# An attention stage on one core: a new order inside each step, value projections in the output bank, and the weighing of values split by query blocks

## The reference, cut to what matters

```python
x = x + 0.5 * ffn(layernorm(x), router_w, gate_w, up_w, down_w)     # 8 experts, top 2
x = x + attn(layernorm(x), W_qkv, W_out)
x = x + 0.5 * ffn(layernorm(x), router_w, gate_w, up_w, down_w)

def attn(x, W_qkv, W_out):                  # x: 8 sequences of 512 tokens, width 128, fp32
    q, k, v = split(x @ W_qkv)              # 16 heads of 64
    q, k = rotary(q), rotary(k)
    s = where(lower_triangle, q @ k.T / 8, -1e9)
    return concat_heads(softmax(s) @ v) @ W_out
```

## Time and profile before

| | |
|---|---|
| time, median of 3 runs | 1277.3 us (1276.87 to 1278.48) |
| profiled execution, first to last instruction | 1277.2 us |
| PE busy | 1203.9 us, 94% |
| DVE busy | 903.4 us, 71% |
| POOL busy | 814.4 us, 64% |
| ACT busy | 795.7 us, 62% |
| first and last matmul of `scores` start (line 2003) | 270.3 us, 1012.7 us |

### The profile page before, as it was taken

The page is one execution under the profiler, slowest core; times in us unless marked ns, Lnnn a source line. Parts: engine busy times, 40 slices in busy tenths (PEclk is TensorE's granted clock), DMA queues, the critical chain, the costliest instruction groups (busy, mean ns, idle before and its releaser), DMA issues. The chain is left out here.

```text
span 1277.2 us, 26829 instructions
## 1 busy us (share of the span) xinstructions
PE 1203.9 (94%) x8070; PEld 891.3 (70%) x8070; DVE 903.4 (71%) x1995; ACT 795.7 (62%) x2264; POOL 814.4 (64%) x888
## 2 busy tenths in 40 slices
PE   7799999979999999999999999999999879999992
PEld 6588888856666666666666666666666568888882
DVE  6775344358888888888788987798998767533543
ACT  4665665646667666767676677766656656555552
POOL 4233356158778788788777776677666536766662
PEclk8899999979999999999999999999999969999996
DMA  9034122122222221222222222212212051114223
GB/s 325 26 96 156 53 57 70 40 66 54 61 46 47 59 59 41 52 59 52 47 52 53 58 54 54 67 34 51 51 36 49 17 180 41 49 48 114 61 63 109
DMA packets 87753, 86.44 MB, mean 68 GB/s; under 512 B 11249, under 2 KB 78705, under 8 KB 87233
## 3 DMA queue, kind: packets, MB, share of 16 engines
q1 hardware_dynamic: 76640, 65.50, 19.9%
q0 software_dynamic: 8864, 18.17, 5.3%
q10 hardware_dynamic: 2112, 1.05, 0.3%
HBM read 33.43 MB, written 17.69 MB: 40 GB/s over the span
## 5 line engine op out<-in xcount | busy, mean ns | idle before, releaser
L1915 POOL TENSOR_SCALAR at_prob<-at_prob,at_rec 128x128 f32<-128x128 f32 (+3 forms) x256 | 312.0, 1223 | 167.6 <-DVE at_rec L2117 165.7
L2297 ACT ACTIVATE at_prob<-at_s,at_nb 128x128 f32<-128x128 f32 (+3 forms) x512 | 264.7, 535 | 16.5 <-DVE at_nb L2109 12.9
L2308 ACT ACTIVATE at_probT<-at_pt 128x128 f32<-128x128 f32 (+3 forms) x256 | 105.2, 437 | 227.5 <-PE at_pt L2022 227.5
L790 POOL DMA_INDIRECT f_xb<-xn_dram,f_source x142 | 141.2, 994 | 161.8 <-PE f_b L1285 101.6
L2109 DVE TENSOR_REDUCE at_nb<-at_s 128x2 f32<-128x256 f32 (+3 forms) x256 | 203.3, 815 | 10.6 <-PE at_s L2008 10.6
L1447 DVE TENSOR_TENSOR f_hid<-f_b,f_silu 128x512 f32<-128x512 f32 x142 | 98.5, 693 | 136.5 <-PE f_b L1298 100.0
L2103 DVE TENSOR_TENSOR at_turned<-at_pj,rope 128x1024 f32<-128x1024 f32 x122 | 148.7, 1219 | 56.5 <-PE at_pj L1969 52.8
L2022 PE MATMUL at_pt<-ident,at_prob 128*128 128x128 f32 x1280 | 183.6, 276 | 4.1 <-DVE wts L381 1.0
L2003 PE MATMUL at_s<-at_KT,at_QT 64*128 64x128 f32 (+3 forms) x1024 | 176.0, 462 | 4.0 <-DMA at_KT<-at_probT 2.8
L1909 POOL TENSOR_TENSOR at_R<-at_turned 128x512 f32<-128x512 f32 x126 | 157.4, 1269 | 24.0 <-DVE at_turned L2103 24.0
L2034 PE MATMUL at_o<-at_probT,at_V 128*64 128x512 f32 (+3 forms) x1024 | 152.0, 437 | 10.9 <-ACT at_probT L2315 3.3
(11 more groups left out here) (326 smaller groups left out, 2224.4 us busy)
## 6 DMA issues: line engine op xcount, KB each, us to landing
at_QT<-at_R SPq DMA_DIRECT2D x128, 128.0 KB, 2.4
at_KT<-at_R SPq DMA_DIRECT2D x124, 128.0 KB, 2.4
ys_dram<-y SPq DMA_DIRECT2D x71, 64.0 KB, 1.8
f_down<-down_t SPq DMA_DIRECT2D x2, 2048.0 KB, 9.2
xn_dram<-f_xn SPq DMA_DIRECT2D x12, 256.0 KB, 6.8
f_xb<-xn_dram,f_source POOLq DMA_INDIRECT x142, 2.6
X<-x SPq DMA_DIRECT2D x4, 512.0 KB, 6.1
gate<-gate_t SPq DMA_DIRECT2D x8, 256.0 KB, 5.1
```

Of the source, the lines that this page charges most:

```text
L790: pool.indirect_dma_start(out=xb[j % AHEAD][:, :], out_offset=None, in_=xn_dram, in_offset=bass.IndirectOffsetOnAxis(ap=routing.source[:, ...
L1915: pool.tensor_scalar(w, w, rec[:, q, 1:2], None, ALU.mult).then_inc(probB_ready, 1)
L2297: act.activation(prob[q][:, h, :], s_bank[q % 2][:, h, 0:n], ACT.Exp, bias=nb[:, q, h:h + 1], scale=1.0, accum_out=sums[:, q, h:h + 1]).th ...
L2308: act.activation(probT[0][:, 0:q + 1, q * P:(q + 1) * P], pt_bank[0][:, at:at + (q + 1) * P].rearrange("p (b r) -> p b r", r=P), ACT.Copy) ...
```

## The change

On PE, the quarter of `values` moves behind the third transposed block and goes to `o_bank` instead of `pj`; it waits for the output of the step before to be copied out of that bank, and `weigh` waits for its copy. The second half of `project` moves from the end of a step to the next step, behind the first transposed blocks. The second scores move in front of `out_project`, and the turns of the input behind both. `weigh` is then the last thing in a step, directly in front of the next scores, and it runs in two parts: query blocks 0 to 2, when those are copied, and then block 3. On DVE the first two maxima stand together at the start, inverting is split from scaling (`invert`) and goes ahead of the copies, the second `rotate` follows the first two copies, the statistics and the first two scalings come before `maximum(i, 2)`, and `residual` comes between `maximum(i, 2)` and `maximum(i, 3)`. On ACT the exponentials of blocks 0 and 1 follow each other, and that of block 2 comes before the copies of block 3. POOL's and SP's lists are as they were.

```diff
@@ -1970,12 +1970,13 @@
 
                 def values(w, t):
                     b, half = w // 2, w % 2
-                    if w == 0 and t % 2:
-                        wait(pe, v_ready, t - 1)
-                        bank = o_bank[:, :]
-                    else:
+                    if w == 0 and t % 2 == 0:
                         projection_bank(v_ready, 4 * w + t + 1)
                         bank = pj[:, :]
+                    else:
+                        wait(pe, v_ready, 4 * w + t - 1)
+                        wait(pe, ot_ready, 4 * (w - 1) + t)
+                        bank = o_bank[:, :]
                     rows = slice(t * P, (t + 1) * P)
                     cols = slice(2048 + half * 512, 2048 + (half + 1) * 512)
                     hi, lo = XT[b % 2][:, 0, rows], XT[b % 2][:, 1, rows]
@@ -2027,13 +2028,22 @@
                     j = i % 8 % 4
                     pe.wait_ge(v_ready, 4 * (i // 4) + 4)
                     wait(pe, ot_ready, i)
+
+                    def heads(b, first, last, start, stop):
+                        for h in range(2):
+                            one = pe.matmul(o_bank[64 * h:64 * h + 64, first:last],
+                                            V[(i // 4) % 2][:, b, 128 * j + 64 * h:128 * j + 64 * h + 64],
+                                            probT[h][:, b, first:last], start=start, stop=stop)
+                        return one
+
+                    pe.wait_ge(ptA_ready, 4 * i + 3)
+                    pe.wait_ge(ptB_ready, 4 * i + 3)
+                    for b in range(3):
+                        heads(b, b * P, 3 * P, b == 0, False)
                     pe.wait_ge(ptA_ready, 4 * i + 4)
                     pe.wait_ge(ptB_ready, 4 * i + 4)
                     for b in range(4):
-                        for h in range(2):
-                            one = pe.matmul(o_bank[64 * h:64 * h + 64, b * P:SEQ],
-                                            V[(i // 4) % 2][:, b, 128 * j + 64 * h:128 * j + 64 * h + 64],
-                                            probT[h][:, b, b * P:SEQ], start=(b == 0), stop=(b == 3))
+                        one = heads(b, 3 * P, SEQ, False, b == 3)
                     one.then_inc(pv_psum, 1)
 
                 for n in range(EARLY):
@@ -2044,6 +2054,7 @@
                         values(0, 2 * n - 1)
                 for i in range(STEPS + 2):
                     this, last = i < STEPS, 0 < i <= STEPS
+                    valued = i > 0 and values_of(i)[0] < HALVES
                     if this:
                         scores(i, 0)
 
@@ -2057,8 +2068,8 @@
                         routing.count_tokens(pe, 0, pt_bank[0][:, 3 * P:4 * P], pt_bank[1][:, 3 * P:4 * P])
                     if last:
                         turn_probs(i - 1, (0, 1))
-                    if i > 0 and values_of(i)[0] < HALVES:
-                        values(*values_of(i))
+                    if 0 < i and i - 1 + EARLY < ROTATIONS:
+                        project(i - 1 + EARLY, 1)
                     if i in LEAD_JUDGED:
                         pe.wait_ge(lead.logits_ready, LEAD_JUDGED[i] + 1)
                     if i == LEAD_COUNTED:
@@ -2066,17 +2077,23 @@
                         pe.wait_ge(routing.gap_ready, 1)
                     if last:
                         turn_probs(i - 1, (2,))
+                    if valued:
+                        values(*values_of(i))
+                    if this:
+                        scores(i, 2)
+                    if i >= 2:
+                        out_project(i - 2)
+                    if valued:
+
+                        last_value = 4 * values_of(i)[0] + values_of(i)[1] + 1
                     if i in TURN:
-
+                        pe.wait_ge(v_ready, last_value)
                         pe.wait_ge(ot_ready, i - 1)
                         prep.turn(pe, TURN[i], o_bank)
                     if i in LEAD_TURNED:
+                        pe.wait_ge(v_ready, last_value)
                         pe.wait_ge(ot_ready, i - 1)
                         lead.turn(pe, LEAD_TURNED[i], prep.xn, o_bank)
-                    if i >= 2:
-                        out_project(i - 2)
-                    if this:
-                        scores(i, 2)
                     if last:
                         turn_probs(i - 1, (3,))
                     if i + EARLY < ROTATIONS:
@@ -2085,10 +2102,10 @@
                         pe.wait_ge(prep.lo_ready, TURN[i])
                     if i in LEAD_TURNED:
                         pe.wait_ge(lead.xts_ready, LEAD_TURNED[i] + 1)
+                    if valued:
+                        pe.wait_ge(v_ready, last_value)
                     if last:
                         weigh(i - 1)
-                    if i + EARLY < ROTATIONS:
-                        project(i + EARLY, 1)
 
             @block.vector
             def _(dve):
@@ -2109,12 +2126,15 @@
                     dve.tensor_reduce(nb[:, q, :], s_bank[q % 2][:, :, 0:(q + 1) * P], axis=AX, op=ALU.max,
                                       negate=True).then_inc(nb_ready, 1)
 
+                def invert(i, q):
+                    Q = 4 * i + q
+                    dve.wait_ge(exp_ready, 2 * Q + 2)
+
+                    wait(dve, probB_ready, Q - 3)
+                    dve.reciprocal(rec[:, q, :], sums[:, q, :]).then_inc(rec_ready, 1)
+
                 def normalise_a(i, q):
                     Q = 4 * i + q
-                    dve.wait_ge(exp_ready, 2 * Q + 2)
-
-                    wait(dve, probB_ready, Q - 3)
-                    dve.reciprocal(rec[:, q, :], sums[:, q, :]).then_inc(rec_ready, 1)
                     dve.wait_ge(rec_ready, Q + 1)
                     w = prob[q][:, 0, :]
                     dve.tensor_scalar(w, w, rec[:, q, 0:1], None, ALU.mult).then_inc(probA_ready, 1)
@@ -2239,37 +2259,40 @@
                     rotate(n, 1)
                 for i in range(STEPS + 2):
                     this, last = i < STEPS, 0 < i <= STEPS
-                    if 0 < i and i - 1 + EARLY < ROTATIONS:
-                        rotate(i - 1 + EARLY, 1)
                     if this:
                         maximum(i, 0)
+                        maximum(i, 1)
                     if last:
-                        normalise_a(i - 1, 3)
-                    if last:
+                        invert(i - 1, 3)
                         copy_b(i - 1, 0)
                         copy_b(i - 1, 1)
                     if i == LEAD_COUNTED:
                         lead_counted(i)
-                    if this:
-                        maximum(i, 1)
+                    if 0 < i and i - 1 + EARLY < ROTATIONS:
+                        rotate(i - 1 + EARLY, 1)
                     if last:
+                        normalise_a(i - 1, 3)
                         copy_b(i - 1, 2)
                     lead_first(i)
+                    if this:
+                        invert(i, 0)
+                        normalise_a(i, 0)
+                        invert(i, 1)
+                        normalise_a(i, 1)
+                    if i in MEASURE:
+                        prep.moments(dve, MEASURE[i])
+                    if this:
+                        maximum(i, 2)
                     if i >= 2:
                         residual(i - 2)
-                    if i in MEASURE:
-                        prep.moments(dve, MEASURE[i])
+                    if this:
+                        maximum(i, 3)
                     if i in TURN:
                         prep.trailing(dve, TURN[i], o_bank)
-                    if this:
-                        normalise_a(i, 0)
-                        normalise_a(i, 1)
-                        maximum(i, 2)
-                    if this:
-                        maximum(i, 3)
                     if i + EARLY < ROTATIONS:
                         rotate(i + EARLY, 0)
                     if this:
+                        invert(i, 2)
                         normalise_a(i, 2)
                     if i < 4:
                         shares(i)
@@ -2283,7 +2306,7 @@
                     if w >= 2 and t == 0:
 
                         act.wait_ge(pv_psum, 4 * (w - 1))
-                    bank = o_bank if w == 0 and t % 2 else pj
+                    bank = pj if w == 0 and t % 2 == 0 else o_bank
                     act.activation(V[w % 2][:, t, :], bank[:, :], ACT.Copy).then_inc(v_ready, 1)
 
                 def exponent(i, q):
@@ -2335,20 +2358,21 @@
                         lead.judged(act, LEAD_JUDGED[i], pt_bank[0][:, 3 * P:4 * P])
                     if this:
                         exponent(i, 0)
+                        exponent(i, 1)
+                    if last:
+                        copy_a(i - 1, 2)
                     if i > 0 and values_of(i)[0] < HALVES:
                         values(*values_of(i))
                     if this:
-                        exponent(i, 1)
+                        exponent(i, 2)
                     if i in TURN:
```

(6 more changed lines are left out.)

## The result

The changed kernel takes 1294.3 us, the median of four runs (1290.8 to 1295.5), against 1277.1 for the kernel before: a ratio of 1.013, 95% interval 1.0115 to 1.0145. It is slower by 17 us; the forecast was 1298. The profiled execution is the shortest of the four, 1290.8 us, with a span of 1289.0.

The account below looks back on a forecast made before the run. PE was taken to set the pace, with DVE only 2.2 us a step to spare. Some 60 steps x 0.13 = 7.8, with 5.6 + 5 + 2.7, made 21 us: 1277.2 + 21 = 1298 us, range 1260 to 1322.

Parts of the forecast that it names:

- The chain: Ordinary attention step from first scores: DVE's held scalings delay `maximum(i, 2)`, `residual` and `project`; 11.71 us, 0.13 more than before.
- The new wait: PE, ready at 7.6 to 8.1 us of the step, waits for `residual`; `project`'s first half starts at 8.49.
- the lower bound: POOL's additions cannot start before the second `rotate` ends: 4.03 to 6.52 us of the step, which then takes 11.53.
- The extras: Moved extra work, seven steps of each kind: `MEASURE` 5.6 us, `TURN` 5, `LEAD_MEASURED` 2.7; routing work counted as no difference.
- The split: PE's `weigh` in two parts: worth 0.76 us a step in the new order, its six added pairs taken at 0.02.
- (a): Rival: DVE's first scaling cannot slip between POOL's two additions; 42 us slower, 1319 us; chance 0.22.
- the seam: Point between POOL's two additions, at 5.46 us of the step, where DVE's scaling of block 0 runs, ending at 5.55.
- (b): Rival: DVE's scalings are not held; step 11.19 us, 1265 us, chance 0.20; full form about 1243 us, chance 0.04.
- (c): Rival: no difference; POOL's additions at their lower bound and half of the extras, +3 us, 1280 us; chance 0.08.
- (d): Rival: POOL's scaling also holds DVE's second scaling; 12.5 us a step, about 1340 us; chance 0.03.
- the prediction's reason against it: In the kernel before, DVE's scaling at 614.49 runs its 0.35 us unhurt inside POOL's scaling from 614.27.

## Why the prediction was right

**The chain.** Predicted and measured times in the ordinary step, t = 0 at the first scores: second `rotate` 2.76, 2.71; additions 4.21 to 6.70, 4.01 to 6.67; scaling of block 0 from 4.97 to 5.55, 4.89 to 5.53; scaling of block 1 until 6.86, 6.82; `maximum(i, 2)` 6.78, 6.74; `residual` done 8.34, 8.29; `project` 8.49, 8.34; `weigh` 9.39, 9.23; next scores 11.71, 11.55. The new wait, its place and both of its causes are as forecast. That `residual`, by way of the held scalings, sets the step is shown by the version that moves them and nothing else.

**What was mis-sized in it.** The restart of `project` behind `residual` took 0.05 us, not the 0.15 that I had from a wait of PE for ACT. With small errors ahead of it (0.05 by the end of `residual`) this makes 0.16 a step, some 9 us over the stage. Two errors inside cancelled: POOL's scaling of block 3 took 1.56 and not 1.85, so the additions began at the lower bound; but the pair took 2.66 and not 2.49, since DVE's scaling of block 3 was under way when it began.

**The extras.** From the starts of the scores in both traces, step by step: the seven `MEASURE` steps are longer by 5.6 us together (predicted 5.6), the seven `TURN` steps by 5.7 (5), the seven `LEAD_MEASURED` steps by 2.7 (2.7). Seventeen other steps from 36 on, mostly with routing work, add 4.4, where I had counted nothing; 21 ordinary ones give back 0.5, the first two 2.6, and the last two add 0.4. The sum is 15.7 to 15.8. How the 17 us between the medians divide beyond that is not shown by two traces that are 11.8 apart. The `TURN` steps are longer for the reason forecast: `weigh` waits for the subtraction and starts at 10.22 of the step (predicted 10.33).

```profile
605.97 0.48 PE L1967 MATMUL at_pj<-at_XT,w_hi 128*128 128x512 f32 x1
...
607.79 2.39 PE L2034 MATMUL at_o<-at_probT,at_V 128*64 128x384 f32 x28 [0.87 <-DVE even_XT L1754]
```

So the three kinds of extras were sized rightly, 14.0 against 13.3 us, and with the routing steps they are the whole loss. That the total of 1298 came out within 4 us is partly luck: the ordinary step, forecast 0.13 longer than before, is 0.03 shorter, which makes the forecast 9 us too high, and the routing steps that it left out make it 4 too low.

**The split.** Predicted at 0.76 us a step in the new order, measured 0.83; its six added pairs at 0.02, measured 0.02.

**The rivals.** (a), the seam lost, did not happen, and the kernel with one addition shows that the seam matters: it costs 13 us to take it away. It is less than the 21 that (a) gave, because the single addition ends at 6.53 of the step, where (a) went by a pair that ends at 6.70; the second scaling is free in both. (b), scalings that are not held, did not happen; its step of 11.19 us is what the version with moved scalings reaches, 11.14. (c) was nearest for the ordinary step: the additions began at 4.01 where it had 4.03, and the step took 11.55 where it had 11.53; it missed by counting half of the extras.

(d), POOL's scaling holding DVE's, did not happen where it was put: the second scaling ends 0.15 after the additions while POOL's own has begun at 616.76. But the prediction's reason against it was misread. POOL's scaling of 128 columns, the first of its two, lasts 0.71 in the kernel before, where DVE's 0.35 starts 0.22 into it, and 0.64 in the changed kernel, where DVE's is over after 0.17; so in the kernel before it was POOL's that got longer.

```profile
614.27 0.71 POOL L1915 TENSOR_SCALAR at_prob<-at_prob,at_rec 128x128 f32<-128x128 f32 x1
616.76 0.64 POOL L1915 TENSOR_SCALAR at_prob<-at_prob,at_rec 128x128 f32<-128x128 f32 x1
```

In other places POOL's scaling does hold DVE's. In the changed kernel's last scaling of 512 columns no addition runs; DVE's starts 0.94 into POOL's, lasts 0.91 instead of 0.48 and ends 0.28 behind it:

```profile
1030.81 1.56 POOL L1915 TENSOR_SCALAR at_prob<-at_prob,at_rec 128x512 f32<-128x512 f32 x1 [0.36 <-DVE at_rec L2134]
1031.75 0.91 DVE L2140 TENSOR_SCALAR at_prob<-at_prob,at_rec 128x512 f32<-128x512 f32 x1
```

And in the kernel before a scaling of block 2 that waits behind another addition of POOL loses to POOL's next scaling, as (d) has it: it takes 1.07 instead of 0.42 and ends 0.77 after the addition (756.87 + 1.28 = 758.15), while on POOL only that scaling runs.

```profile
758.12 1.25 POOL L1915 TENSOR_SCALAR at_prob<-at_prob,at_rec 128x384 f32<-128x384 f32 x1
757.85 1.07 DVE L2120 TENSOR_SCALAR at_prob<-at_prob,at_rec 128x384 f32<-128x384 f32 x1
```

The Trainium skill (SBUF — State Buffer, section SBUF: two separate sides) counts DVE instructions in a two-port mode among those that take the pair they share with GpSimd, whichever starts first. The held scaling and copy agree, and so do the additions that are 0.17 us longer behind a scaling and the scaling of 0.91 us above; if the first is the one that the profile shows to start first, the 0.35 us scaling that starts 0.22 into POOL's does not bear it out.

**What stays open.** Why a scaling stays held when its elements are interleaved, and whether DVE's or POOL's scaling gives way when the two meet. Scalings and copies from SBUF to SBUF are held, reciprocals and row statistics are not; what in the instruction decides was not settled.

## What to carry to other kernels

When an engine's list is reordered, lay it beside the list of the engine that it shares something with: here two scalings whose hold cost nothing where they stood were moved so that both fall into POOL's additions, in front of the instruction that sets the pace. Of a changed order that gives nothing, test the parts alone: the split gave 11 us by itself, the whole change lost 17, and moving two lines gave 39. And a wait that disappears from one engine should be looked for at the next use of the buffer that it guarded.

## What the runs showed of the hardware

- DVE's scaling and copy from SBUF to SBUF wait for the end of a two-operand addition of POOL and end 0.09 us behind it at 128 columns; they can slip in between two such additions that follow each other without a gap. A reciprocal of 128 columns (952 to 954 ns, 128 times) and row statistics (0.27 to 0.29 us inside additions, 54 times in the kernel before) are not held.
- It works in the other direction too: two additions that begin while such a scaling runs take 2.66 us instead of 2.49, and POOL's scaling of 512 columns takes 1.56 instead of 1.85 when no scaling of DVE starts beside it.
- POOL's scaling can hold DVE's as well: one of 512 columns that starts 0.94 into POOL's of 512 takes 0.91 us instead of 0.48. One of 256 that starts 0.22 into POOL's of 128 keeps its 0.35, and POOL's takes 0.71 instead of 0.64.
- Fourteen pairs of small matmuls, each with its own weight load, take 2.32 us where eight pairs with the same columns took 2.30.
